# A recurrence and a mixture of experts on one core: the filler matmuls of TensorE in the steps of the narrow pair tiles

## The reference

```python
xW = x @ Wx + b
h[t] = tanh(xW[t] + h[t-1] @ Wh)              # 1024 steps, one after the other
logits = h @ gate_w.T                         # top 2 of 8 experts, softmax over the two
hidden = silu(h @ wg[e].T) * (h @ wu[e].T)    # for each expert e
y = sum over e of combine[e] * (hidden @ wd[e].T)
out = x + y
```

## Time and profile before

| | |
|---|---|
| median of 3 runs | 838.35 us (835.32 to 840.39) |
| the profiled execution's own time | 838.66 us |
| its span, first to last instruction | 836.8 us |
| mean granted clock | 0.901 |
| PE, PEld, ACT, DVE busy | 781.6, 752.9, 528.2, 448.6 us |
| L565, the fillers | 511 matmuls, 163.9 to 760.8 us |

### The profile page before, as it was taken

How to read it: one execution, slowest core, us unless ns; L and a number is a source line. 1 busy time by engine, 2 the same in 40 slices (tenths; PEclk the granted TensorE clock), 3 DMA queues, 4 the chain that set the end, 5 groups by cost and what they waited for, 6 DMA issues and landing times.

```text
span 836.8 us, 51689 instructions
## 1 busy us (share of the span) xinstructions
PE 781.6 (93%) x21958; PEld 752.9 (90%) x21958; DVE 448.6 (54%) x2582; ACT 528.2 (63%) x2845; POOL 146.5 (18%) x140
## 2 busy tenths in 40 slices
PE   8777777899999999999999999999999999999894
PEld 5666666799999999999999999999999999998894
DVE  4777768445454545454544545454545545456452
ACT  5777878566666656665666656665666666565452
POOL 1000000102012210302021111212031232215232
PEclk8555555599999999999999999999999999999998
DMA  5777766501111111211111111111011111112111
GB/s 140 196 197 197 202 190 180 183 10 35 24 31 29 32 23 20 42 17 36 21 39 24 26 27 26 34 23 36 17 37 24 30 29 23 29 21 42 30 30 24
DMA packets 35764, 49.65 MB, mean 59 GB/s; under 512 B 5808, under 2 KB 22192, under 8 KB 35504
## 3 DMA queue, kind: packets, MB, share of 16 engines
q1 hardware_dynamic: 27200, 36.53, 15.8%
q0 software_dynamic: 8064, 9.58, 7.9%
q10 hardware_dynamic: 272, 0.26, 0.1%
HBM read 35.57 MB, written 12.88 MB: 58 GB/s over the span
## 4 chain that ended last, share of the span: by engine, by line
PE 82%; ACT 5%; DVE 4%; DMA 3%; issue 3%; POOL 0%; POOLq 0%; DVEq 0%; ACTq 0%
PE bank L534 26%; PE bank L450 18%; PE bank L614 16%; PE bank L556 13%; ACT h L780 3%; DVE lo L1092 3%; PE bank L565 3%; DMA arena<-w_all 2%; PE bank L427 2%; PE bank L513 1%; DMA out<-y_sb,place_now 1%; PE bank L505 1%; ACT w_hi L765 1%; PE bank L641 1%; ACT rows L715 1%
## 5 line engine op out<-in xcount | busy, mean ns | idle before, releaser
L1092 DVE TENSOR_TENSOR lo<-h,hi 128x4 f16<-128x4 f32 x1024 | 168.6, 165 | 340.8 <-ACT h L780 326.8
L772 ACT ACTIVATE hi<-bank 128x4 f16<-128x4 f32 x1024 | 177.5, 173 | 223.5 <-PE bank L450 192.4
L614 PE MATMUL bank<-lo,wh_hi 128*128 128x2 f16 x4096 | 258.5, 167 | 30.9 <-DVE lo L1092 27.4
L450 PE MATMUL bank<-hi,wh_hi 128*128 128x2 f16 x4096 | 252.1, 165 | 5.3 <-ACT hi L772 4.4
L450 PE MATMUL bank<-hi,wh_lo 128*128 128x2 f16 x4096 | 246.1, 164 | 0.2
L614 PEld LDWEIGHTS bank<-lo,wh_hi 128*128 128x128 f16 x4096 | 175.0, 99 | 47.5 <-DVE lo L1092 43.9
L450 PEld LDWEIGHTS bank<-hi,wh_hi 128*128 128x128 f16 x4096 | 199.8, 99 | 10.1 <-ACT hi L772 7.1
L780 ACT ACTIVATE h<-bank 128x4 f32<-128x4 f32 x1024 | 177.3, 173 | 35.0 <-PE bank L614 31.6
L450 PEld LDWEIGHTS bank<-hi,wh_lo 128*128 128x128 f16 x4096 | 177.9, 97 | 0.5 <-issue 0.3
L534 PE MATMUL bank<-x_T,w_hi 128*128 128x64 f16 (+1 forms) x2048 | 156.4, 203 | 2.2 <-ACT arena L737 1.2
L556 PE MATMUL bank<-arena,w_hi 128*128 128x64 f16 (+1 forms) x1792 | 143.4, 205 | 0.3 <-issue 0.2
(11 more groups left out here) (145 smaller groups left out, 1178.7 us busy)
## 6 DMA issues: line engine op xcount, KB each, us to landing
arena<-w_all SPq DMA_DIRECT2D x96, 256.0 KB, 3.1
xrow<-expert_rows SPq DMA_DIRECT2D x82, 66.0 KB
early<-xT SPq DMA_DIRECT2D x17, 128.0 KB
expert_rows<-pad SPq DMA_DIRECT2D x8, 132.0 KB
expert_rows<-rows,slot POOLq DMA_INDIRECT x64
out<-y_sb,place_now POOLq DMA_INDIRECT x32, 3.1
out<-y_sb,place_wide POOLq DMA_INDIRECT x24
arena<-wh_in ACTq DMA_DIRECT2D x1, 256.0 KB, 4.0
```

The lines of the kernel that those rows point to most:

```text
L450: mm = pe.matmul(preact(n)[:, B * m:B * m + B], w[:, k, m * P:(m + 1) * P], hi[:, blk % 2, k, B * tt:B * tt + B], start=False, stop=False, ...
L614: mm = pe.matmul(preact(n)[:, B * m:B * m + B], wh_hi[:, k, m * P:(m + 1) * P], lo[:, pi, k, B * pt:B * pt + B], start=False, stop=False, ...
L772: act.activation(hi[:, blk % 2, :, B * tt:B * tt + B], src, ACT.Tanh, scale=1 / SCALE).then_inc(s_hi, 1)
L1092: v.tensor_tensor(lo[:, i, :, B * tt:B * tt + B], h32[:, 4 * (tt % 2):4 * (tt % 2) + 4].rearrange("p (c b) -> p c b", c=2), hi[:, i, :, B ...
```

## The change

`keep_warm` is called with 14 units as before where the step's pair tile is a wide one, and with 0 units, so no filler at all, in the steps of the ten narrow pair tiles. The first six steps are wide and keep 24.

```diff
                 if p >= 0:
-                    keep_warm(free_cols(o), (FIRST_UNITS if n < START + FIRST_STEPS else UNITS) - units)
+                    keep_warm(free_cols(o), (FIRST_UNITS if n < START + FIRST_STEPS else UNITS if wide(p) else 0) - units)
```

## The result

The changed kernel took 836.06 us (median of 15 runs), the kernel before, measured beside it, 839.27 us (15 runs). The ratio is 0.9966, with a 95% interval of 0.9952 to 0.9981: 0.34% or 2.9 us faster, a small gain, clear of noise and under the 0.5% of the forecast.

What follows compares the result with a forecast made beforehand. A loop over VectorE, TensorE and ScalarE, about 0.72 us a step, was the bound. Late steps (0.5) and pauses (1.2) give 1.7 us: 838.66 - 1.7 - 0.3 = 836.6 us, range 832.5 to 841.0.

Steps and rivals of the forecast that it cites:

- the 0.5% of the forecast: Limit of 4.2 us under which the small gain was forecast to stay, with a chance of 0.74.
- the lo loop: Narrow steps: VectorE's `lo`, TensorE's four lo products and ScalarE's tanh close in 0.72 us and set the step.
- the sign that the prediction had named: Narrow steps: L614 waits for VectorE's `lo`, or TensorE idles 0.03 to 0.06 us a step ahead of it.
- TensorE's 6.0 us: TensorE's row in narrow steps: time of the 143 removed fillers, claimed gain 0; rival that all comes out, chance 0.12.
- The pauses: Narrow stretch: 13 TensorE waits with no releaser, 2.9 us, each to shrink by 0.09 us with fewer instructions; 1.2 us.
- The 0.5 us from late steps: Narrow steps where TensorE, ScalarE or VectorE is late: removing the filler gives an earlier start; 0.5 us.
- The clock: Narrow stretch: clock stays at 1.00 without fillers; rival that it falls and the kernel slows by over 0.5%, chance 0.14.
- The price: Narrow step at clock 0.50: twelve products 0.64 us plus 0.36 for the recurrence's twelve and L427, given as 1.03 us.
- short falls at 1.0 us each: Narrow stretch: a clock fall as long as the one at 784.4 us costs 3.3 steps, 1.0 us.
- The starting point: Whole kernel before the change: median of the runs 838.35 us, from which the gain was taken.
- 836.6: Forecast time in us of the whole changed kernel, after a gain of 1.7 us.

Runs made afterwards that it cites:

- split kernel: Kernel before with each 128-column product of the wide tiles made as two of 64, the same weights loaded twice; ratio 1.0251.
- the kernel with fillers and standstill: Kernel before plus 20 extra ScalarE copies in step 840, each waiting for the last, so TensorE stands still some 5 us; 918.22 us.

## Why the prediction was right

- **What bounds the step.** Right: the lo loop at 0.717 us. Shown by the clean narrow stretch (28 steps in 20 us, unchanged), by the 0.02 to 0.05 us that TensorE now waits ahead of L614 in steps of 0.717 us, which is the sign that the prediction had named, and by the kernel without any fillers, whose wide steps at 1.00 keep 139 in 100 us.
- **TensorE's 6.0 us are not gained.** Right. With as many columns and 141 products fewer the gain is there; with 2 columns in each filler it isn't.
- **The pauses.** The mechanism was right: they belong to the instruction stream, at a fixed count of instructions, behind a packet that comes late. The term was 1.2 us, from shrinking 13 pauses by 0.09 us each. In the first two profiles the excess of the steps over 0.86 us fell from 4.3 us (17 steps) to 0.7 us (3 steps), 3.6 us. That can't be taken as the size of the term, since the second profile of the changed kernel has 13 steps with 4.3 us. What sizes it are the medians: the whole gain was 2.9 us on the first chip for the 1.7 predicted, 3.7 on another, and 3.8 with one product fewer. So the term was too small by 1 to 2 us. One reason shows: I took the 2.9 us of the list of waits as all that the pauses cost, while the steps over 0.86 us hold 4.3 us. Whether pauses shrink or vanish no run tells apart.
- **The 0.5 us from late steps.** Not shown apart; it lies inside the noise.
- **The clock.** The price was right, 1.03 us a step measured and predicted. The two terms that it names, 0.64 and 0.36, make 1.00; the 0.03 that is left must stand for L427, for which it gives no figure. "The clock stays at 1.00" was right for 26 of 27 runs of the changed kernel. That the narrow fillers guard it could not be shown: the kernel before lost it in 2 of 86 runs (861.1 and 912.1 us). What was wrong is the picture of short falls at 1.0 us each. With fillers or without, the fall that I forced in this stretch lasted until the recurrence ended.
- **The starting point.** The median of before was 839.27 over 15 runs and not the 838.35 of three. That 836.6 came within 0.5 us of 836.06 is luck: a start that was 0.9 us too low made up for a gain that was too small.

Still open is why the clock falls in a few runs. The kernel with fillers of 2 columns lost it in 3 of 12 runs, those with one or three products fewer and full columns in 0 of 24, the one without any fillers in 3 of 4, and the split kernel in 1 of 4. The counts are too small to tell a cause. Open is also why packets take longer in one run than in another, and whether that is what differs between chips.

## What to carry to other kernels

Where TensorE runs weight load and product in pairs that each cost 0.025 to 0.03 us, count instructions, not only time: a pause of 0.2 to 0.4 us at multiples of 256 instructions with no releaser is the instruction stream, and one product less per step makes such pauses fewer. Read this from the median of many runs, since the pauses of one profile vary by as much as the change. Taking a product away gains only what the pauses cost if something else, here a loop over three engines, sets the step; and where a block lasted 4.7 us there was no pause to gain. Judge fillers by many runs, too: what they guard against shows in one run of ten or of forty, not in the median.

## What was unexpected of the hardware

- Pauses of TensorE at multiples of 128 pairs, where a block is used up in 3.7 to 3.9 us and not where it lasts 4.7: none in the wide stretch of the kernel before, 42 with 15.2 us in the same stretch of the split kernel. The first instruction behind a pause starts 1.2 to 1.7 us after the end of a packet of queue q8.
- TensorE busy for 100 of 100 us at 2,396 products (700 to 800 us of the kernel with fillers and standstill) kept a granted clock of 0.50 once it had fallen; steps of the same make had held 1.00 ahead of the standstill. In the wide stretch without fillers the clock came back after 208 us.
- Two chips of the same type differ by 0.5% on the same kernel, 838.9 and 843.5 us.
